# Cross-attention's context transposed by VectorE instead of TensorE, with two smaller moves in the same step

## What is computed

```python
B, T, D, TC = 16, 112, 512, 375          # batches, text tokens, channels, context tokens
a = layer_norm(ctx, ln_gamma, ln_beta)   # over the 512 channels of each context token
Q, K, V = x @ Wq.T, a @ Wk.T, a @ Wv.T   # 16 heads of 32
scores = where(mask, (Q . K) * 32**-0.5, -inf)
x1 = x + tanh(gate) * (softmax(scores) @ V) @ Wo.T
out = rwkv_block(x1, state taken from ctx)   # not touched
```

## Time and profile before

| | |
|---|---|
| median of 3 runs | 1399.43 us (1397.38 to 1405.21) |
| profiled execution, its own time | 1399.84 us |
| its span | 1398.0 us |
| PE, DVE, ACT, POOL busy | 94%, 67%, 54%, 38% |
| TensorE clock granted, mean | 0.979 |

### The profile page before, as it was taken

How to read it: one execution, slowest core, us unless ns; L and a number is a source line. 1 busy time by engine, 2 the same in 40 slices (tenths; PEclk the granted TensorE clock), 3 DMA queues, 4 the chain that set the end, 5 groups by cost and what they waited for, 6 DMA issues and landing times.

```text
span 1398.0 us, 42906 instructions
## 1 busy us (share of the span) xinstructions
PE 1319.0 (94%) x17120; PEld 936.5 (67%) x17120; DVE 939.5 (67%) x2416; ACT 752.2 (54%) x1804; POOL 528.5 (38%) x582
## 2 busy tenths in 40 slices
PE   6999999999999999897899999999999999999967
PEld 5777777777777777666666666766676666667624
DVE  3555555555555555547578888888888789887852
ACT  4776677676676677532434453445444544454342
POOL 2221112222222222113547545654566355644550
PEclk9999999999999999987899999999999999999978
DMA  7333322222222222213000010010100010000000
GB/s 228 100 105 107 98 63 69 75 71 70 65 76 76 76 69 92 63 50 136 15 14 22 22 28 14 23 27 21 24 14 26 21 28 11 25 21 21 8 15 14
DMA packets 39402, 73.48 MB, mean 53 GB/s; under 512 B 17781, under 2 KB 20469, under 8 KB 37701
## 3 DMA queue, kind: packets, MB, share of 16 engines
q1 hardware_dynamic: 39237, 71.01, 17.2%
HBM read 60.01 MB, written 7.57 MB: 48 GB/s over the span
## 4 chain that ended last, share of the span: by engine, by line
PE 73%; DVE 13%; issue 8%; ACT 2%; DMA 2%; POOL 1%; SPq 1%; DVEq 0%; POOLq 0%; ACTq 0%
PE b_bank L2017 15%; PE b_bank L2023 12%; PE ring_bank L703 7%; PE ring_bank L704 6%; PE ring_bank L705 6%; PE av_bank L789 4%; PE score_banks L762 4%; DVE probs L450 3%; PE b_bank L2132 3%; PE score_banks L749 3%; PE b_bank L2158 2%; DVE bv L1404 2%; DVE probsT L467 2%; PE av_bank L775 2%; DVE ktil L1398 1%
## 5 line engine op out<-in xcount | busy, mean ns | idle before, releaser
L1139 POOL TENSOR_TENSOR rst<-rp,st 128x448 f32<-128x448 f32 x192 | 202.5, 1078 | 34.9 <-DVE st L1425 32.0
L450 DVE CUSTOM_DVE_ANT_0 probs<-score_banks,unmask 112x375 f32<-112x375 f32 x256 | 124.9, 545 | 93.0 <-issue 93.0
L595 ACT ACTIVATE probs<-probs,least_inv 112x375 f32<-112x375 f32 x256 | 152.7, 609 | 32.5 <-DVE least_inv L450 32.5
L467 DVE SCALAR_TENSOR_TENSOR probsT<-score_banks,least_cols 125x448 f32<-125x448 f32 x192 | 108.0, 618 | 54.2 <-PE score_banks L762 51.8
L610 ACT ACTIVATE probsT<-probsT,key_mask 125x448 f32<-125x448 f32 x192 | 114.7, 662 | 47.6 <-DVE probsT L467 47.4
L1131 POOL TENSOR_TENSOR xm<-mixed,xa 128x448 f32<-128x448 f32 x80 | 89.6, 1129 | 96.1 <-DVE mixed L1354 90.7
L375 POOL TENSOR_TENSOR ctx_rstd<-ctx_var_eps,a_eps_exp 125x3 f32<-125x3 f32 x16 | 13.9, 866 | 272.7 <-DVE ctx_var_eps L423 272.7
L340 POOL TENSOR_TENSOR aT_lo<-whole,aT_hi 128x375 fp32r<-128x375 f32 x64 | 59.0, 922 | 152.3 <-ACT whole L576 150.2
L703 PE MATMUL ring_bank<-aT_hi,wk_lo 128*128 128x376 f32 x256 | 91.2, 356 | 0.9 <-issue 0.9
L1159 POOL TENSOR_TENSOR cen_r<-wkv,sq_r 128x448 fp32r<-128x448 f32 x15 | 17.1, 1140 | 196.6 <-ACT sq_r L1829 196.6
L1354 DVE SCALAR_TENSOR_TENSOR mixed<-b_bank,vec_sb,sx 128x112 f32<-128x112 f32 x320 | 82.5, 324 | 5.6 <-POOL xm L1131 3.9
(11 more groups left out here) (197 smaller groups left out, 3156.6 us busy)
## 6 DMA issues: line engine op xcount, KB each, us to landing
least_cols<-values_of_two_batches SPq DMA_DIRECT2D x32, 437.5 KB
ctx_tok<-in_ctx SPq DMA_DIRECT2D x16, 672.0 KB
xT_sb<-in_xT SPq DMA_DIRECT2D x16, 224.0 KB, 3.0
inv_cols<-values_of_two_batches SPq DMA_DIRECT2D x128, 28.0 KB, 3.7
x_tok<-in_x SPq DMA_DIRECT2D x16, 224.0 KB, 2.7
x_between_layers<-x_tok SPq DMA_DIRECT2D x16, 224.0 KB, 4.6
b_x<-x_between_layers SPq DMA_DIRECT2D x16, 224.0 KB, 2.6
out_dram<-ln_tok SPq DMA_DIRECT2D x16, 224.0 KB, 2.3
```

What stands on the lines that cost most here:

```text
L450: dve.tensor_tensor_reduce(out=probs[:, g % 2, i], in0=score_bank[0:T, i, 0:TC], in1=unmask[:, m[1]], scale=-SCALE, scalar=-LOWEST, op0=AL ...
L467: dve.scalar_tensor_tensor(out=probsT[:, g % 2, k].rearrange("p (i t) -> p i t", t=T), in0=score_bank[0:TK, :, k * T:(k + 1) * T], scalar= ...
L595: act.activation(probs[:, g % 2, i], probs[:, g % 2, i], ACT.Exp, scale=-1.0, bias=least_at(m, g, i), accum_out=sums[:, g, i:i + 1]).then_ ...
L1139: pool.tensor_tensor(by_chunk(rst[:, j % NPROD]), by_chunk(rp[:].rearrange("p c t -> p (c t)")), state_of(j), ALU.mult).then_inc(s_pprod, 1)
```

## The change

1. From batch 1 on PE no longer turns the context. `load_quads` loads each batch a second time, as `ctx_quads`: 128 partitions made of four groups of 32, one for each 128 channels, in eight DMAs per batch (four of 32 partitions by 11 runs of 512 bytes, four of 23 partitions). DVE's `turn_ctx` transposes blocks of 32 by 32 into `ctxT` with four instructions. As tokens now lie along the free axis, mean and reciprocal root are spread over all partitions through DRAM (`spread_stats`, two DMAs, the second 128 partitions by 2 by 375 values), and DVE subtracts (`centre_ctx`, two instructions) and multiplies (`scale_ctx`, two). ACT applies gamma and beta in place (`affine_aT`), then rounds into `aT_hi` (`copy_aT`).
2. Batch 0 is still turned by PE (`apply_first`, `transpose_first`, `affine_first`).
3. `scores(n, 2)` stand inside the last value product: chunks 0 and 1 of V2, the scores, chunks 2 and 3.
4. The query comes in three parts, `qa` and `qb` of one chunk and `qc` of two; `ctx_tok` has one buffer instead of two; `ln_stats` moves to the start of DVE's step.
5. `least_cols` comes in two DMAs, of 112 and 13 partitions.
6. Channels lie in another order, so `wk` and `wv` are loaded in four DMAs of 32 partitions each, gamma and beta in eight small ones, and PE waits for these too. Tokens lie in natural order, so the key mask is read byte by byte.

```diff
-RING = ["K0", "S1", "K1", "K2", "K3", "V0", "V1", "V2", "S0", "T0", "T1", "T2", "T3", "qa", "qb"]
+RING = ["K0", "S1", "K1", "K2", "K3", "V0", "V1", "V2", "S0", "qa", "qb", "qc"]
+QUERY = {"qa": (0, 1), "qb": (1, 2), "qc": (2, 4)}
...
+    def load_quads(sp, b):
+        if at_least(b, 2):
+            sp.wait_ge(s_turned, count(later(b, -2), 1, 1))
+        else:
+            sp.wait_ge(s_ring, unit_done((-1, 1), f"T{C - 1}"))
+        tokens = A["ctx"][index(b)]
+        for q in range(QUADS):
+            channels, rows = slice(q * P, (q + 1) * P), q * BLOCK
+            sp.dma_start(ctx_quads[rows:rows + BLOCK, 0:TB - 1],
+                             tokens[0:TC - TAIL, channels].rearrange("(k r) d -> r k d", r=BLOCK)).then_inc(s_quads, 16)
+            sp.dma_start(ctx_quads[rows:rows + TAIL, TB - 1], tokens[TC - TAIL:TC, channels]).then_inc(s_quads, 16)
...
+        def spread_stats(b):
+            sp.wait_ge(s_rstd, count(b, 1, 1))
+            sp.dma_start(stats_in_dram(b).rearrange("a (p k) -> p a k", k=KT), meanvar[:]).then_inc(s_stat_out, 16)
+            sp.wait_ge(s_stat_out, count(later(b, -1), 16, 16))
+            sp.dma_start(stat_rows[:], stats_in_dram(b).rearrange("(o a) t -> o a t", o=1).broadcast_to([P, 2, TC])).then_inc(s_stat_in, 16)
...
-        sp.dma_start(key_mask8[:], A["mask"].rearrange("b (p k) -> p b k", p=TK),
+        sp.dma_start(key_mask8[:], A["mask"].rearrange("b (k p) -> p b k", p=TK),
                      allow_slow_non_contiguous=True).then_inc(s_w["key_mask"], 16)
-        sp.dma_start(wo[:], A["wo"]).then_inc(s_w["wo"], 16)
+        load_quads(sp, (0, 1))
...
+        def turn_ctx(b):
+            dve.wait_ge(s_quads, count(later(b, -1), 32 * QUADS, 32 * QUADS))
+            dve.wait_ge(s_split, count(later(b, -1), C, C))
+            for c in range(C):
+                last = dve.transpose(ctxT[:, c].rearrange("p (k r) -> p k r", r=BLOCK), ctx_quads[:, :, c * BLOCK:(c + 1) * BLOCK])
+            last.then_inc(s_turned, 1)
...
+            if normalise:
+                ln_stats(later(n, 1))
             if attend:
                 invert_sums(m, 1)
...
             if attend:
                 shift_scores(m, 0)
+            if normalise:
+                turn_ctx(later(n, 1))
             if project:
                 mask_scores(n, 0, range(HG))
+            if normalise and not is_batch(n, 0):
+                centre_ctx(later(n, 1))
             if is_batch(n, 0):
                 split_weight("wv", wv_lo, wv_hi, 1)
             if attend:
                 shift_scores(m, 1)
             if normalise:
-                ln_stats(later(n, 1))
+                if is_batch(n, 0):
+                    centre_ctx(later(n, 1))
+                scale_ctx(later(n, 1))
...
             if project:
-                project_value(n, 2)
+                project_value(n, 2, range(2))
                 scores(n, 2)
+                project_value(n, 2, range(2, C))
                 turn_rows(n, 0)
             if normalise:
-                for c in range(3):
-                    transpose_ctx(p, c)
+                project_query(p, "a")
             if attend:
                 weigh_values(m, 2)
                 key_major_scores(m, 3)
...
             if normalise:
-                transpose_ctx(p, 3)
-                project_query(p, "a", (0, 1))
+                project_query(p, "b")
             if project:
                 scores(n, 3)
             if attend:
                 weigh_values(m, 3)
             if normalise:
-                project_query(p, "b", (2, 3))
+                project_query(p, "c")
```

More of the change, by code:

```diff
@@ new lines, in centre_ctx, with scale_ctx @@
+        def centre_ctx(b):
+            dve.wait_ge(s_stat_in, count(later(b, -1), 16, 16))
+            dve.wait_ge(s_turned, count(later(b, -1), 1, 1))
+            for h in range(2):
+                part = ctxT[:, 2 * h:2 * h + 2, 0:TC]
+                dve.tensor_tensor(part, part, stat_rows[:, 0:1].broadcast_to([P, 2, TC]), ALU.subtract).then_inc(s_cent, 1)
+        def scale_ctx(b):
+            for h in range(2):
+                dve.wait_ge(s_cent, count(later(b, -1), 2, h + 1))
+                part = ctxT[:, 2 * h:2 * h + 2, 0:TC]
+                dve.tensor_tensor(part, part, stat_rows[:, 1:2].broadcast_to([P, 2, TC]), ALU.mult).then_inc(s_ctxn, 1)
@@ L530, in step @@
                 mask_scores(n, 1, range(HG))
-            if normalise:
-                ln_apply(later(n, 1))
             if is_batch(n, B - 1):
@@ L654, in step @@
                 act.activation(tanh_gate[:], gate[:], ACT.Tanh).then_inc(s_gate, 1)
+            if normalise:
+                for c in range(C):
+                    affine_aT(p, c)
             if attend:
@@ L661, in step @@
             if normalise:
-                for c in range(3):
+                for c in range(C):
                     copy_aT(p, c)
+                copy_query(p, "a")
             if attend:
@@ L674, in step @@
             if normalise:
-                copy_query(p, "b", slice(2, 4))
+                copy_query(p, "c")
+        for c in range(C):
+            affine_first(c)
         for c in range(C):
@@ L679, in scalar @@
         round_weight(W["wk"], wk_hi, "wk")
[L680 to L681 removed]
+        for part in "abc":
+            copy_query((0, 0), part)
         run(act, step)
@@ L726, in project_value, with project_query @@
                                 c == 0, c == C - 1)
-            last.then_inc(s_ring, 1)
-        def project_query(b, part, chunks):
+            if C - 1 in chunks:
+                last.then_inc(s_ring, 1)
+        def project_query(b, part):
             if is_batch(b, 0):
                 pe.wait_ge(s_w["wq"], 16)
-            dst = free_unit(*query_unit(b, part))
+            n, name = query_unit(b, part)
+            dst = free_unit(n, name)
             pe.wait_ge(s_xT[b[1]], 16 * (b[0] + 1))
-            for i, m in enumerate(chunks):
+            for i, m in enumerate(range(*QUERY[name])):
                 for c in range(C):
```

178 lines of the change are left out of this document (106 added, 72 removed).

## The result

The changed kernel takes 1418.78 us (median of 4 runs, 1417.87 to 1420.7), the kernel before 1400.49 us beside it (4 runs, 1397.38 to 1405.21): ratio 1.0138 [1.0116, 1.0159]. The forecast was 1404 with a range from 1391 to 1415, so the time lies outside it, on the slower side. The profiled execution took 1418.93 us.

A forecast was written before the change was run, and what follows sets the result against it. PE's own queue was taken to bound attention. Terms -7.0 (14 steps), -2.5 (step 0), +12 and +2 (start) gave +4.5 us on 1399.84, so 1404, range 1391 to 1415: no change, leaning to slower.

The forecast's parts named there:

- The start: Before batch 0's first masks: DVE waits for batch 1's second load, 12 us later, V0 likewise; 2 us more for PE's restart.
- The byte packets: Key mask load at the start: read byte by byte, 6000 packets instead of 2000, 4.6 us more.
- The start is dearer: Rival, chance 0.28: loads into 32 partitions run at half rate, start +20, sum +10.5, 1410 us.
- From SP's release to the turning: Start: SP held until about 29.9 us, batch 1's second load landing between 35.7 and 38.3, taken as 36.
- The waits named for the start: Start: DVE idle before the transposes until a DMA ends; SP held behind the key mask until about 29.9 us.
- step 0: First attention step, without key-major scores: PE's own queue gives some 4.3 us, third scores 1.4 earlier, 2.5 us less.
- The step: Steady attention step: 0.5 us less each, 7 us over 14 steps, bounds 0.3 to 0.7.
- Now the third scores come after 1.6: PE's steady step: third scores 1.6 us after V2's start (half of V2 and its gap), instead of 2.97.
- the wait at the fourth scores: PE's steady step: a new wait of 1.1 us for DVE's shift of the key-major scores.
- the full 1.8 us: PE's steady step: 1.53 us of transposes plus 0.30 of mask wait, not expected to go together; rival's chance 0.05.
- DVE, ACT and SP in the steady state: Steady step: DVE's transposes (1.9 us) and centring (1.8) fit idle time; ACT and SP have room; nothing on DVE is paid.
- The spread of the maxima in two parts: Loading least_cols: shortens a transfer DVE waited for once in the trace, 1.5 us, so worth nothing.

The follow-up runs named there:

- e2: The changed kernel with wk and wv each loaded in one DMA over 128 partitions instead of four over 32: 1414.35 us.
- e9: The changed kernel with 3.1 us more of useless DVE work per batch, ahead of the turning and the centring: 1418.01 us.
- e4: The kernel before with only least_cols loaded in two parts, 112 and 13 partitions: 1395.79 us against 1398.5.
- e1: The changed kernel with the key mask stored in DRAM as 125 rows of 48 bytes, 125 packets instead of 6000: 1405.76 us.

## Why the prediction was wrong

**The start: the mechanism was right, its size was not.** I forecast +12 us with bounds of 1.9 and 21; it was +22.1 at V0. Its three terms:

- *The byte packets.* I took "4000 more, 4.6 us", that is some 1.2 ns for a packet whatever it holds, from the earlier trace rows. They took 1.84 ns, and the mask 10.9 us (27.4 to 38.3) instead of 2.6 + 4.6 = 7.2: 3.7 us. Why single bytes are slower than three was not tested; the trace has a third of them at 25 or 26 ns and the others at 9, where nearly all of the three-byte packets took 9. The upper bound of 21 us allowed for a byte costing double and was still too low, since it left the quarters out.
- *The loads by quarters.* They were a rival ("The start is dearer", chance 0.28) and not part of the sum. The mask's packets began 4.2 us later (27.4 instead of 23.2), and e2 brought them and the turning forward by as much (4.5 and 4.3 us). I had reckoned 5.2. I had treated as a choice between cases what was a term of its own; and the rule of the Trainium skill that the rival cites spoke for it.
- *From SP's release to the turning.* 6.1 us forecast (29.9 to 36), 8.3 measured (37.9 to 46.14): 2.2 us. I took the time of the first load for it; here one DMA engine alone works for the last 2 us, as the window from 44 to 45.5 us shows. That this engine serves the DMAs of 23 partitions is likely and not shown.

Together 3.7 + 4.2 + 2.2 = 10.1 us, which is what the term was short. The waits named for the start (DVE ahead of the transposes, released by a DMA; SP behind the key mask) are in the trace. Two neighbours held: V0 to the second scores took 5.09 instead of 2.97 us at the 1.2 GHz level (I had added 2), and step 0 won 22.1 + 2.1 - 21.5 = 2.7 us by its fourth scores (forecast 2.5).

**The step: 0.5 us forecast, 0 measured. This is the term that failed in kind.** "Now the third scores come after 1.6" counted V2's half alone. But the third scores also wait for a shift, that of the same group (`shift_scores(m, 2)`), 2.83 us behind the key-major scores ahead of V2 (382.02 to 384.85 here). I had worked out exactly this distance for the fourth scores (k + 2.83, as in the earlier trace rows) and did not ask it of the third. They come 0.3 us later for the wait, and the rest is lost in tenths behind both waits: second to third scores 7.40 against 7.0, third to fourth 7.01 against 6.91, fourth to projection 3.48 against 3.37. Right were the wait at the fourth scores (1.1 forecast, 1.05 measured), the end of the one ahead of the key-major scores, and that the full 1.8 us would not be had. From the fourth scores of batch 0 to those of batch 14, the 14 steps took 507.16 us before and 507.22 now: +0.1 instead of -7.0.

**DVE, ACT and SP in the steady state: right.** The turning as it stands in a step:

```profile
401.55 1.95 DVE L491 STREAM_TRANSPOSE ctxT<-ctx_quads 128x384 f32<-128x384 f32 x4
405.29 0.54 DVE L523 CUSTOM_DVE_ANT_0 probs<-score_banks,unmask 112x375 f32<-112x375 f32 x1 [1.79 <-issue]
...
407.16 1.79 DVE L499 TENSOR_TENSOR ctxT<-ctxT,ctx_stat_rows 128x750 f32<-128x750 f32 x2
```

It takes 1.95 us for four (1.9 forecast), 1.79 of idle time left behind it out of the 3.66 in the earlier trace rows, and 1.79 for the centring (1.8). e9 shows that there was 3 us more room. For ACT and SP the evidence is that nothing waited for them: from 200 to 500 us PE's own waits are for DVE alone.

**The spread of the maxima in two parts: wrong, small.** I called it "nothing" since the earlier trace rows show one wait of 1.5 us. That wait lay in the last attention step, where PE stood behind it with nothing else to do; one wait in the whole trace can be paid in full. The changed kernel's last stretch is 2.5 us shorter, and e4 has all of it alone.

**The sum as it came:** 22.06 (V0) + 2.12 (clock) - 2.69 (step 0) + 0.06 (14 steps) - 0.41 (the last batch's step) - 2.51 (spread) + 0.17 (the rest) = 18.80 us, against 4.5. Of the 14.3 us missed the start has 10.1 and the 14 steps 7.1; the spread goes the other way.

## What to carry to other kernels

When an instruction is moved on a queue that waits for other engines, list every input that it waits for at the new place and time each from its producer, not the one that was late at the old place only. When PE has two gaps that wait on DVE, its spare work must be dealt out between them: here each of two moves was worth nothing alone and 12 to 14 us together. At the start, a DMA of tiny runs charges whoever stands behind it on the queue, so ask what has come to stand there; lay small tables out on the host in the tile's order, and load large ones into all partitions at once.

## What was not expected of the hardware

- A DMA of single bytes took 1.84 ns per packet, one of three-byte runs 1.21, and SP was held 23.02 us in the next issue. Lengthening the runs to 48 bytes (e1) took 9.5 us off the start.
- Loads into 32 partitions at a time ran at 218 GB/s where whole ones had 410 and 401.
- The second load of batch 1 ended with some 2 us in which one of the 16 DMA engines worked alone, at 19 GB/s (44 to 45.5 us).
- After 19.25 us without work PE was granted 0.50 of its clock, and its matmuls took 0.63 instead of 0.39 us for the next 4.5 us of work, not more than 2.1 us in all: much idle time cost little beyond itself.
- A spread to 125 partitions, cut into parts of 112 and 13, was no longer waited for. The Trainium skill's page "DMA: Bandwidth & Descriptors", section "Why a DMA increments its semaphore by 16 and not by 1", says that the number of engines is the largest one up to 16 that divides the slowest dimension on both sides; that is 5 for 125, 16 for 112 and 13 for 13. The packets agree with it: 4.9 engines at work before, 10.9 on average in e4, and 2.1 instead of 4.3 us for a spread.
